# The two lowest merge levels of a block inverse on narrow tiles of 32 columns

## The reference

```python
def step(S, inp):
    qt, kt, vt, gt, bt = inp
    S = S * jnp.exp(gt)[..., None, None]
    mem = jnp.einsum('bhk,bhkv->bhv', kt, S)
    delta = (vt - mem) * bt[..., None]
    S = S + jnp.einsum('bhk,bhv->bhkv', kt, delta)
    o = jnp.einsum('bhk,bhkv->bhv', qt * scale, S)
    return (S, o)
```

## Time and profile before

| | |
|---|---|
| median of 3 runs | 2520.83 us (2520.28 to 2522.46) |
| profiled execution, its own time | 2518.24 us |
| its span, first to last instruction | 2516.3 us |
| mean granted TensorE clock | 0.978 of full speed |
| delta rule, line 1135, first and last start | 120.2 and 2127.7 us |

### The profile page before, as it was taken

How to read it: one execution, slowest core, us unless ns; L and a number is a source line. 1 busy time by engine, 2 the same in 40 slices (tenths; PEclk the granted TensorE clock), 3 DMA queues, 4 the chain that set the end, 5 groups by cost and what they waited for, 6 DMA issues and landing times. The chain is left out here.

```text
span 2516.3 us, 53535 instructions
## 1 busy us (share of the span) xinstructions
PE 2352.5 (93%) x18800; PEld 1889.7 (75%) x18800; DVE 2004.9 (80%) x4146; ACT 1407.4 (56%) x3331; POOL 1279.2 (51%) x2046
## 2 busy tenths in 40 slices
PE   6599999999999999999999999999999998699997
PEld 2378888888888888888888888888888887546665
DVE  5678888888888888888888888888888887235544
ACT  3256666666666666666666666666666665322221
POOL 3456566666666666666666666656566665100000
PEclk9689999999999999999999999999999999799998
DMA  4211121112111211121112111211121110221100
GB/s 129 69 36 35 27 61 34 34 33 55 35 36 36 54 37 35 36 54 36 36 36 55 36 36 36 55 36 36 36 55 36 36 26 9 66 62 34 34 9 9
DMA packets 203849, 103.20 MB, mean 41 GB/s; under 512 B 97009, under 2 KB 185018, under 8 KB 203586
## 3 DMA queue, kind: packets, MB, share of 16 engines
q1 hardware_dynamic: 203266, 99.65, 17.0%
q10 hardware_dynamic: 320, 0.13, 0.0%
HBM read 69.89 MB, written 2.54 MB: 29 GB/s over the span
## 5 line engine op out<-in xcount | busy, mean ns | idle before, releaser
L861 DVE SCALAR_TENSOR_TENSOR dr_y<-dr_ps,cw,dr_y 128x255 f32<-128x255 f32 (+2 forms) x1152 | 479.9, 472 | 8.9 <-ACT dr_y L986 8.9
L1125 POOL TENSOR_TENSOR dr_fo<-dr_vo,dr_nhalf 128x4 f32<-128x4 f32 x128 | 156.1, 1219 | 539.5 <-DVE dr_vo L941 539.5
L744 PE MATMUL dr_ps<-dr_w,dr_am 128*128 128x96 f32 x3072 | 418.1, 280 | 3.2 <-ACT dr_w L1038 3.2
L744 PEld LDWEIGHTS dr_ps<-dr_w,dr_am 128*128 128x128 f32 x3072 | 380.3, 193 | 12.1 <-ACT dr_w L1038 3.9
L831 DVE TENSOR_TENSOR dr_w<-dr_ps,mask 128x512 bf16<-128x512 f32 x512 | 350.3, 684 | 31.4 <-PE dr_ps L629 24.6
L986 ACT ACTIVATE dr_y<-dr_ps,cw 128x256 f32<-128x256 f32 x384 | 160.9, 470 | 195.1 <-PE dr_ps L676 195.0
L1038 ACT COPY dr_w<-dr_ps 128x384 f32<-128x384 f32 x384 | 188.8, 492 | 134.8 <-PE dr_ps L744 134.8
L972 ACT CAST dr_tn<-dr_ps 128x512 bf16<-128x512 f32 x384 | 226.3, 589 | 55.7 <-PE dr_ps L644 55.6
L873 DVE TENSOR_TENSOR_SCAN dr_dec<-dr_abc,dr_dg 128x512 f32<-128x512 f32 x128 | 208.4, 1628 | 33.4 <-POOL dr_dg L1091 18.1
L975 ACT CAST dr_tt<-dr_ps 128x512 bf16<-128x512 f32 x384 | 233.5, 608 | 0.0
L650 PE MATMUL dr_ps<-dr_tt,dr_w 128*128 128x128 bf16 x2048 | 197.9, 219 | 20.1 <-DVE dr_w L831 20.1
(11 more groups left out here) (204 smaller groups left out, 5059.9 us busy)
## 6 DMA issues: line engine op xcount, KB each, us to landing
dr_abc<-scr_a SPq DMA_DIRECT2D x64, 512.0 KB, 5.4
dr_qk<-dr_sy SPq DMA_DIRECT2D x384, 48.0 KB, 2.0
dr_bcb<-scr_b SPq DMA_DIRECT2D x128, 64.0 KB, 4.6
dr_c<-dr_b SPq DMA_DIRECT2D x512, 4.0 KB, 1.8
dr_qk<-dr_sy SPq DMA_DIRECT2D x128, 32.0 KB, 1.9
ex_modb<-scr_mod SPq DMA_DIRECT2D x4, 1024.0 KB, 8.1
wv<-in_Wv SPq DMA_DIRECT2D x8, 384.0 KB, 3.5
wo<-in_Wo SPq DMA_DIRECT2D x1, 3072.0 KB, 12.1
```

The lines of the kernel that those rows point to most:

```text
L744: last = pe.matmul(ps[:, bank, h * DV:(h + 1) * DV], wt(h), x[:, h * DV:(h + 1) * DV], start=(start and h == 0), stop=(h == QH - 1), skip_ ...
L861: v.scalar_tensor_tensor(y[:, slot, x:T], ps[:, BANK[n], off:off + T - x], cw[:, t, TAPS - 1 - x:TAPS - x], y[:, slot, x:T], ALU.mult, ALU ...
```

## The change

NARROW = 2 levels now run on tiles of 32 columns per unit, and LEVELS falls to 2 (block sizes 32 and 64, LVL0 = 5). A narrow level multiplies the block-diagonal part of b16 (`b32`, made by the new GpSimd piece `block`) by c32t: 8 matmuls of 32 columns. VectorE masks the 256 columns into w32 (`narrow1`). TensorE multiplies tt by w32, ScalarE copies the 256 columns back to c32t (`narrow2`). VectorE's `widen` gets the other orientation from it by its transpose of 32x32 blocks (c32) and spreads it to tt; after the second narrow level it spreads c32t to tn too. `expand` spreads tt alone.

PLAN is written anew for all pieces. Folded, the part around the change reads: ... delta 0 1, acc 1, negate 0, decayed 1 0, decayed 1 1, negate 1, scores 1, expand, state_out | gate 0, ks, narrow1 0, mean 0, gate 1, narrow2 0, widen 0, w0 1, gated 0, proj 0, narrow1 1, taps 0 0, residual 1 0, narrow2 1, proj 1, keys_gain, delta 1 0, widen 1, oT 0, merge1 0 0, taps 0 1, root, keys_scale, residual 1 1, merge2 0 0, merge1 0 1, wo 0, taps 1 0, values 0, silu 0, merge2 0 1, merge1 1 0, acc 0, delta 1 1, round 0, taps 1 1, proj 2, values 1, merge2 1 0, silu 1, merge1 1 1, out 1, merge2 1 1, taps 2 0, block, w0 0, norms, mean 1, taps 2 1, gains, residual 0 0, silu 2, rows, keys, gated 1, ... The pieces gate, block and round belong to stage 1 now.

```diff
@@ -45,8 +45,9 @@
 STEPS = NQ * B
 U = CH * QH
 BASE = 8
-LEVELS = 4
-LVL0 = 3
+NARROW = 2
+LEVELS = 2
+LVL0 = 5
 DEPTH = 4
...
@@ -618,10 +627,7 @@
             def merge1(st, l, g):
                 it, m = st
                 if l == 0:
-                    pe.wait_ge(s["te_ok"], it * 2 + 1)
-                    if g == 0:
-                        pe.wait_ge(s["ab_ok"], it + 1)
-                        wait(pe, s["tt_ok"], (it * LEVELS - 1) * 2 + 1 if it else 0)
+                    pe.wait_ge(s["te_ok"], it * (NARROW + 2) + NARROW + 1)
                 else:
                     pe.wait_ge(s["tt_ok"], (it * LEVELS + l - 1) * 2 + g + 1)
                     pe.wait_ge(s["tn_ok"], (it * (LEVELS - 1) + l - 1) * 2 + g + 1)
@@ -634,7 +640,7 @@
...
                 pe.wait_ge(s["mask_ok"], (it * LEVELS + l) * 2 + g + 1)
                 if l == 0:
-                    pe.wait_ge(s["te_ok"], (it + 1) * 2)
+                    pe.wait_ge(s["te_ok"], (it + 1) * (NARROW + 2))
                 if g == 0:
                     wait(pe, s["tt_ok"], (it * LEVELS + l) * 2 if not isinstance(it, int) or it or l else 0)
                 middle = l < LEVELS - 1
...
                 last.then_inc(s["bc_ps"], 1)
+
+            def narrow1(st, l):
+                it, m = st
+                if l == 0:
+                    pe.wait_ge(s["ab_ok"], it + 1)
+                    pe.wait_ge(s["b32_ok"], (it + 1) * CH)
+                    pe.wait_ge(s["c32t_ok"], it * (NARROW + 1) + 1)
+                else:
+                    pe.wait_ge(s["cn_ok"], it * NARROW + l)
+                for u in range(U):
+                    last = pe.matmul(ps[:, X0, u * 4 * BASE:(u + 1) * 4 * BASE], b32[:, u, :], c32t[:, u, :],
+                                     start=True, stop=True)
+                last.then_inc(s["n1_ps"], 1)
+
+            def narrow2(st, l):
+                it, m = st
+                pe.wait_ge(s["wn_ok"], it * NARROW + l + 1)
+                pe.wait_ge(s["te_ok"], it * (NARROW + 2) + l + 1)
+                if l == 0:
+                    wait(pe, s["tt_ok"], it * LEVELS * 2)
+                for u in range(U):
+                    last = pe.matmul(ps[:, X1, u * 4 * BASE:(u + 1) * 4 * BASE], tt[:, u, :], w32[:, u, :],
+                                     start=True, stop=True)
...
 
+            def spread(dst, src):
+                blk = bc(bd32[:].rearrange("p (n i) -> p n i", i=4 * BASE), 1, U)
+                return v.tensor_tensor(wide(dst[:]), bc(src[:], 2, 4), blk, ALU.mult)
+
+            def turned(dst, src):
+                return v.transpose(dst[:].rearrange("p u i -> p (u i)"), src[:].rearrange("p u i -> p (u i)"))
+
             def expand(st):
                 it, m = st
                 v.wait_ge(s["xb_ok"], it + 1)
+                wait(v, s["te_ok"], it * (NARROW + 2))
                 v.tensor_tensor(c32[:].rearrange("p u (r i) -> p u r i", r=4), bc(xb[:], 2, 4),
                                 bc(bc(const[:, C_QUART:C_QUART + 4], 1, U), 3, BASE), ALU.mult).then_inc(s["c32_ok"], 1)
                 v.wait_ge(s["c32_ok"], it + 1)
-                v.transpose(c32t[:].rearrange("p u i -> p (u i)"), c32[:].rearrange("p u i -> p (u i)")
-                            ).then_inc(s["c32t_ok"], 1)
+                turned(c32t, c32).then_inc(s["c32t_ok"], 1)
                 wait(v, s["p3"], it * LEVELS * 2)
-                blk = bc(bd32[:].rearrange("p (n i) -> p n i", i=4 * BASE), 1, U)
-                v.wait_ge(s["c32t_ok"], it + 1)
-                v.tensor_tensor(tn[:].rearrange("p u (n i) -> p u n i", i=4 * BASE), bc(c32t[:], 2, 4), blk,
-                                ALU.mult).then_inc(s["te_ok"], 1)
-                v.tensor_tensor(tt[:].rearrange("p u (n i) -> p u n i", i=4 * BASE), bc(c32[:], 2, 4), blk,
-                                ALU.mult).then_inc(s["te_ok"], 1)
+                spread(tt, c32).then_inc(s["te_ok"], 1)
+
+            def narrow1(st, l):
+                it, m = st
+                v.wait_ge(s["n1_ps"], it * NARROW + l + 1)
+                wait(v, s["n2_ps"], it * NARROW + l)
+                v.tensor_tensor(w32[:], ps[:, X0, 0:NCOL].rearrange("p (u n) -> p u n", u=U), bc(maskn[:, l, :], 1, U),
+                                ALU.mult).then_inc(s["wn_ok"], 1)
+
+            def widen(st, l):
+                it, m = st
+                v.wait_ge(s["cn_ok"], it * NARROW + l + 1)
+                v.wait_ge(s["te_ok"], it * (NARROW + 2) + l + 1)
+                if l == NARROW - 1:
+                    spread(tn, c32t).then_inc(s["te_ok"], 1)
+                turned(c32, c32t).then_inc(s["c32t_ok"], 1)
+                v.wait_ge(s["c32t_ok"], it * (NARROW + 1) + l + 2)
+                spread(tt, c32).then_inc(s["te_ok"], 1)
 
             def taps(st, n, part):
...
                 act.copy(dst, ps[:, (X0, X2)[g], :].rearrange("p (u n) -> p u n", u=QH)).then_inc(s["tt_ok"], 1)
+
+            def narrow2(st, l):
+                it, m = st
+                act.wait_ge(s["n2_ps"], it * NARROW + l + 1)
+                act.wait_ge(s["c32t_ok"], it * (NARROW + 1) + l + 1)
+                act.copy(c32t[:], ps[:, X1, 0:NCOL].rearrange("p (u n) -> p u n", u=U)).then_inc(s["cn_ok"], 1)
...
                 pool.tensor_tensor(heads, heads, bc(fo[:], 2, DV), ALU.mult).then_inc(s["gf_ok"], 1)
+
+            def block(st):
+                it, m = st
+                wait(pool, s["n1_ps"], it * NARROW)
+                for c in range(CH):
+                    us = slice(c * QH, (c + 1) * QH)
+                    pool.wait_ge(s["b16_ok"], it * CH + c + 1)
+                    pool.tensor_tensor(b32[:, us, :], b16[:, m, us, :], bc(bd32[:], 1, QH), ALU.mult).then_inc(s["b32_ok"], 1)
...
     c[:, C_IOTA:C_IOTA + E] = np.arange(E)
+    for l in range(NARROW):
+        size, col = BASE << l, i // (4 * BASE) * (4 * BASE)
+        at = col[:, None] + np.arange(4 * BASE)
+        same = i[:, None] // (2 * size) == at // (2 * size)
+        other = i[:, None] // size != at // size
+        c[:, C_NARROW + l * 4 * BASE:C_NARROW + (l + 1) * 4 * BASE] = (same & other) | (i[:, None] == at)
```

More of the change, by code:

```diff
@@ L61 @@
 ATANH = [1.0 / (2 * k + 1) for k in range(9)]
[L63 to L70, removed]
[5 rows of a table removed]
[L76 to L80, removed]
@@ new lines @@
+PLAN = ((1.72, ("proj", 0)), (2.58, ("taps", 0, 0)), (3.61, ("proj", 1)), (4.52, ("taps", 0, 1)),
+        (4.96, ("taps", 1, 0)), (5.37, ("silu", 0)), (7.54, ("taps", 1, 1)), (7.65, ("proj", 2)),
+        (8.07, ("silu", 1)), (8.42, ("taps", 2, 0)), (9.29, ("norms",)), (9.37, ("taps", 2, 1)), (9.6, ("gains",)),
+        (9.75, ("silu", 2)), (10.14, ("keys",)), (10.67, ("decays", 0)), (11.0, ("scores", 0)),
+        (12.1, ("decayed", 0, 0)), (12.18, ("decayed", 0, 1)), (12.74, ("decays", 1)), (13.28, ("negate", 0)),
+        (13.4, ("decayed", 1, 0)), (13.49, ("decayed", 1, 1)), (13.79, ("negate", 1)), (14.29, ("scores", 1)),
+        (15.27, ("gate", 0)), (15.61, ("gate", 1)), (18.68, ("keys_gain",)), (19.54, ("root",)),
+        (19.6, ("keys_scale",)), (20.23, ("values", 0)), (22.13, ("round", 0)), (22.8, ("values", 1)),
+        (23.53, ("block",)), (24.9, ("rows",)), (25.89, ("base",)), (29.53, ("expand",)), (30.44, ("narrow1", 0)),
[4 rows of a table added]
+        (42.17, ("residual", 0, 1)), (42.79, ("delta", 0, 1)), (44.53, ("state_out",)), (45.39, ("ks",)),
+        (45.54, ("mean", 0)), (45.89, ("w0", 1)), (45.91, ("gated", 0)), (48.16, ("residual", 1, 0)),
+        (49.04, ("delta", 1, 0)), (49.14, ("oT", 0)), (49.62, ("residual", 1, 1)), (49.76, ("wo", 0)),
+        (50.67, ("acc", 0)), (51.75, ("delta", 1, 1)), (53.14, ("out", 1)), (54.36, ("mean", 1)),
+        (55.31, ("gated", 1)), (55.67, ("oT", 1)), (57.78, ("wo", 1)), (57.8, ("acc", 1)))
@@ L87 @@
 C_BD = C_UNIT + BASE
-C_COLS = C_BD + P
+C_NARROW = C_BD + P
+C_COLS = C_NARROW + NARROW * 4 * BASE
 def wait(eng, sem, value):
@@ L539, in slots @@
                     on[piece[0]](stages[k], *piece[1:])
+        NCOL = U * 4 * BASE
+        wide = lambda ap: ap.rearrange("p u (n i) -> p u n i", i=4 * BASE)
         def run(eng, on):
@@ L547, in delta_rule @@
         PIECES = ("merge1", "merge2", "w0", "delta", "residual", "ks", "out", "state_out", "mean", "gated", "oT", "wo",
-                  "acc", "rows", "base", "expand", "proj", "silu", "taps", "gate", "norms", "gains", "root", "keys_gain", "decays", "keys", "keys_scale", "scores", "decayed", "negate",
+                  "acc", "rows", "block", "base", "expand", "narrow1", "narrow2", "widen", "proj", "silu", "taps", "gate", "norms", "gains", "root", "keys_gain", "decays", "keys", "keys_scale", "scores", "decayed", "negate",
                   "values", "round")
@@ L662, in rows_ @@
                 last.then_inc(s["bc_ps"], 1)
+            def narrow1(st, l):
[19 more added lines that the diff above has]
+                                     start=True, stop=True)
+                last.then_inc(s["n2_ps"], 1)
```

(8 more changed lines are left out.)

7 lines of the change are left out of this document (6 added, 1 removed), and 9 rows, old and new, of the table PLAN.

## The result

The changed kernel takes 2629.5 us (median of 4 runs, 2628.8 to 2631.1) against 2520.9: 1.043 times the time before, 95% interval 1.041 to 1.045. The direction was forecast, the time was not: 2629.5 lies above the range of 2500 to 2615. The profiled execution's span is 2627.4 us, 111 more than before.

A forecast was written before the change was run, and what follows sets the result against it. TensorE nearest its limit, VectorE second, the step a closed loop of waits: 11.46 us mean 1 to expand plus 21.3 back, taken as 32.7, +0.87 us over 62 steps, adding 54 us: 2574 us, range 2500 to 2615.

The forecast's parts named there:

- wait (a): VectorE between the copies of S and ks: nothing left to do while TensorE makes the ks product, 1.0 us.
- The loop of waits: Whole step: a closed loop of queue waits, not the larger engine sum; 32.7 us, chance 0.58 for 2574 us.
- wait (b): VectorE between narrow1 0 and widen 0: only mean 0 to do while TensorE finishes gate 1, 0.86 us.
- closes by TensorE as well: TensorE from ks product to out 1: 16.8 us work, 0.8 waits, ending within 0.2 us of VectorE's path.
- GpSimd's chain: GpSimd from mean 1 through fo, gate scaling, dg, copy and fourteen products: makes VectorE wait at expand, 11.46 us.
- Narrow matmuls: TensorE's added 32-column matmuls: 0.036 us each, 32 of them 1.15 us a step, bounds 0.4 to 1.8.
- Block: GpSimd's new piece before mean 1: two products, 2.04 us, bounds 1 and 4, hidden by its wait there.
- Spreads: VectorE's added spreads of tt: two at 1.04 us; 0.36 taken off for the last one of widen 1.
- rival D: Shared port: widen's spreads wait for whole GpSimd instructions, 0.5 to 1.0 us a step more, 2610 to 2640; chance 0.13.
- B's condition: Rival with waits covered: decided if mean 1 to expand falls below 10.5 us; 2465 us, chance 0.22.
- The 0.71 for slower: Whole kernel: chance that the change makes it slower, from the main forecast and the shared-port rival together.

The follow-up runs named there:

- the filled variants: Changed kernel with unneeded TensorE matmuls added right before ks waits for S: 4 gave 2601.6 us, 12 gave 2563.3, 32 gave 2565.1.
- gate 1 later: Changed kernel with gate 1 moved behind narrow2 0 in PLAN: 2718.5 us, ratio 1.079 against the kernel before.
- the last run: Version with S ahead of expand and gated 0 behind narrow1 1, plus the copy that starts base moved to block: 2397.8 us, ratio 0.951.
- the place of S: Changed kernel with state_out one place earlier in PLAN, ahead of expand: 2454.3 us, ratio 0.973 against the kernel before.

## Why the prediction went wrong

**The step that failed** is the one at wait (a): "TensorE too stands still here: gate 0 has ended some 2.9 us before S is ready, so its relief is spent at this place." The standstill was found (2.25 us long in the trace) and priced at nothing beyond the lost relief. The runs put its price at 64 us of the 109: filling it, the queue untouched, brings the kernel to 2563, which is 11 under the forecast of 2574. All rows of the kernel before that the sum rests on were taken at a granted clock of 1.00; that a standstill of a length which the steady steps before never had (their longest was 1.16 us, once) could change the level was not among the bounds. The Trainium skill (TensorE: Matmul & The Clock Gate, Why this matters for your kernels) tells to avoid long idle gaps between bursts of matmuls because the clock drops after them. The trace agrees with the drop (2.69 against 1.54 us for gate 1), not with the length, for the page speaks of gaps longer than the 2.25 us that were enough here; the measurement decides. A drop of the clock should have been a rival with a chance of its own.

**The loop of waits** was right where the clock stayed up, in 8 of 63 steps and nearly all of the filled variants: 32.7 us a step, mean 1 to expand 11.6 (11.46 forecast), expand to mean 1 21.1 (21.3), waits of 1.09, 1.01 and 0.82 us. With the clock down wait (b) grew to 1.97. That it closes by TensorE as well was right: mean 1 still waits 0.21 us for the squares that come from out 1, and a shorter wait (b) gained nothing (gate 1 later). So was that GpSimd's chain sets expand's start (the last run).

**Removed and added work** was mis-sized in terms whose errors nearly cancel in the step. Narrow matmuls: their groups' successors come after 0.20 to 0.22 us, 0.026 each, not 0.036 (32 of them 0.8 us, not 1.15), below the 0.03 to 0.045 that was to show it. Block took 2.28 us, not 2.04, and stayed hidden. Spreads:

```profile
L866 DVE TENSOR_TENSOR dr_tt<-dr_c,bd x192: 647/692/1323, 127.7 to 2256.9; 128x1024 bf16<-128x1024 bf16 x192
L866 DVE TENSOR_TENSOR dr_tn<-dr_c32t,bd x64: 674/686/965, 136.0 to 2255.8; 128x1024 bf16<-128x1024 bf16 x64
```

The median record is 0.69 us, where 1.04 was taken for each and a cheap one for the last alone; in the step shown three are at 0.65 to 0.69 and the one of widen 0 at 1.32. Part of the saving came back, as expand's first product takes 0.83 instead of 0.42. The product and the spread of 1.32 us both start less than 0.1 us behind a GpSimd instruction that still runs, which fits the mechanism of rival D; no run here isolates it.

**Rivals.** D forecast 2610 to 2640, and the time lies there by luck: its steps of 33.3 to 33.7 at full clock never came, three of the four spreads are cheap, and filling the standstill takes the time to 2563 with the spread of 1.3 us in place. B's condition, mean 1 to expand below 10.5 us, was not met in any version (11.2 at the least); what made the kernel faster was first of all the place of S. The 0.71 for slower stands on the right mechanism, since the kernel is slower by 42 us without the clock too, and lacked one term.

## What to carry to other kernels

When an engine is relieved, ask where in the queue its new idle time collects. If it is TensorE and the time collects in one place, add to the price what the following matmuls cost at the lower clock, and try a place for the released wait, or even useless work, before giving the change up. Read an order written out by hand pair by pair: two pieces of one engine with another engine's answer between them (S, then ks) need something to do in between.

## What the runs showed of the hardware

One standstill of 2.25 us in a step of 33.9 was enough for the granted clock to fall to the level of 1.2 GHz, from 0.2 us before its end to 1.6 us after it, though TensorE was busy for 90% of the step; at 2.04 us left it fell in a bit over half of the steps (one run), at 1.59 in none of the steady ones. The length alone doesn't decide: in the 8 steps of 32.7 us of the changed kernel the clock stayed up beside the same standstill, and with the narrow levels in the old order most steps (38 of 63) show no loss beside one of 2.26 us. What decides there stays open.

A GpSimd copy of 128x64 took 1.17 us beside VectorE's scan and 0.24 without it. Eight bf16 matmuls of 32 columns, each with its own 128-wide weights, took 0.20 us from start to the next group's start.
